# A two-phase convolution and FFN kernel: two images packed into one convolution, and the last image's search, broadcast and additions rearranged

## The reference, cut to what matters

```python
x = x + relu(batchnorm(conv3x3(sign(ln_c(x)), sign(w) * alpha) + b))   # ln_c over channels, batch statistics over all images
t = tokens(x)                                  # (32, 3136, 128)
s = ln_t(t)
weights = s @ wr + br                          # one router weight per token
sel = top (k - 1) of weights, k = 3136 / 2     # per image
t = t + s + (gelu(s[sel] @ w1 + b1) @ w2 + b2) * weights[sel]   # the last term for chosen tokens alone
```

## Time and profile before

| | us |
|---|---|
| median of 3 runs | 2095.73 |
| lowest, highest | 2092.15, 2099.53 |
| the profiled execution | 2102.06 |
| its span | 2100.1 |
| TensorE, VectorE, ScalarE, GpSimd busy | 1961.1, 1600.5, 1216.2, 938.0 |
| first convolution pass begins | 19.9 |
| last convolution pass ends | 471.5 |
| last matmul of the second phase ends | 2079 |

### The profile page before, as it was taken

The page is one execution under the profiler, slowest core; times in us unless marked ns, Lnnn a source line. Parts: engine busy times, 40 slices in busy tenths (PEclk is TensorE's granted clock), DMA queues, the critical chain, the costliest instruction groups (busy, mean ns, idle before and its releaser), DMA issues.

```text
span 2100.1 us, 35007 instructions
## 1 busy us (share of the span) xinstructions
PE 1961.1 (93%) x9515; PEld 961.7 (46%) x9515; DVE 1600.5 (76%) x4580; ACT 1216.2 (58%) x2030; POOL 938.0 (45%) x714
## 2 busy tenths in 40 slices
PE   6999999994999999999999999999999999999995
PEld 2444444442444444444444444444444444444442
DVE  4766666665788888888888888887888888878875
ACT  3555555544666666666666666666656666655652
POOL 1000000005465565566555566655656566555543
PEclk9999999996999999999999999999999999999998
DMA  6787877852133333333333333333333333333223
GB/s 251 279 297 283 301 291 288 295 215 73 52 141 117 115 116 132 114 126 117 126 112 135 116 112 120 135 113 113 130 119 117 123 115 122 116 112 129 96 76 119
DMA packets 78097, 318.24 MB, mean 152 GB/s; under 512 B 23561, under 2 KB 28610, under 8 KB 74050
## 3 DMA queue, kind: packets, MB, share of 16 engines
q1 hardware_dynamic: 64626, 265.07, 34.5%
q10 hardware_dynamic: 13392, 52.33, 6.7%
HBM read 237.88 MB, written 78.26 MB: 151 GB/s over the span
## 4 chain that ended last, share of the span: by engine, by line
PE 48%; DMA 11%; SPq 6%; DVE 4%; issue 4%; POOL 1%; ACT 1%; ACTq 0%; POOLq 0%; DVEq 0%
PE ps L1063 24%; DMA y<-y_int 6%; PE ps L1052 6%; PE ps L1054 5%; PE ps L1053 5%; PE ps L1008 5%; SPq L429 4%; DMA w_row<-wrow 3%; PE ps L1041 2%; DMA wse<-w_row 2%; SPq L435 1%; POOL rm L489 1%; ACT hs L566 1%; SPq L440 1%; DVE rm L776 1%
## 5 line engine op out<-in xcount | busy, mean ns | idle before, releaser
L1063 PE MATMUL ps<-hs,w_c 128*128 128x448 f32 x1792 | 765.1, 555 | 0.6 <-ACT yo L576 0.6
L566 ACT ACTIVATE hs<-ps,b1c,undo 128x448 f32<-128x448 f32 x896 | 609.3, 719 | 129.0 <-PE ps L1054 125.3
L1063 PEld LDWEIGHTS ps<-hs,w_c 128*128 128x128 f32 x1792 | 314.6, 191 | 211.3 <-issue 177.2
L965 PE MATMUL ps<-yo,cwT 128*128 128x448 bf16 x2016 | 396.2, 357 | 3.9 <-ACT y L544 3.9
L470 POOL TENSOR_TENSOR xb<-xb,zr 128x448 f32<-128x448 f32 x224 | 261.1, 1168 | 271.9 <-ACT zr L594 254.9
L475 POOL TENSOR_TENSOR tl<-tr,th 128x448 f16<-128x448 f32 x224 | 245.4, 1097 | 306.9 <-PE ps L1054 185.8
L1052 PE MATMUL ps<-th,w_h 128*128 128x448 f16 x896 | 318.7, 356 | 25.3 <-ACT hs L566 25.3
L1054 PE MATMUL ps<-th,w_l 128*128 128x448 f16 x896 | 316.3, 353 | 0.0
L1053 PE MATMUL ps<-tl,w_h 128*128 128x448 f16 x896 | 316.3, 353 | 0.0
L482 POOL TENSOR_TENSOR yo<-yo,base 128x448 f32<-128x448 f32 x224 | 281.3, 1262 | 77.4 <-DVE yo L885 77.4
L965 PEld LDWEIGHTS ps<-yo,cwT 128*128 128x128 bf16 x2016 | 193.8, 98 | 214.4 <-issue 24.9
(11 more groups left out here) (143 smaller groups left out, 2086.1 us busy)
## 6 DMA issues: line engine op xcount, KB each, us to landing
xb<-x SPq DMA_DIRECT2D x21, 1568.0 KB, 7.4
xb<-x SPq DMA_DIRECT2D x33, 896.0 KB, 4.7
gate_all<-gate_row ACTq DMA_DIRECT2D x32, 896.0 KB, 4.5
result<-yo SPq DMA_DIRECT2D x32, 896.0 KB, 3.5
y_int<-y SPq DMA_DIRECT2D x32, 784.0 KB, 4.1
xb<-x SPq DMA_DIRECT2D x33, 672.0 KB, 4.4
gate_all<-gate_row ACTq DMA_DIRECT2D x32, 672.0 KB, 5.6
result<-yo SPq DMA_DIRECT2D x32, 672.0 KB, 3.0
```

Of the source, the lines that this page charges most:

```text
L566: nc.scalar.activation(hs[(b + slot) % 2][:, j, :], ps[:, H_BANK + j, 0:T], ACT.Gelu_apprx_tanh, bias=b1c[:, j:j + 1], scale=undo[:, 1:2]) ...
L965: last = M(bank, cwT[:, t, :], sg[b][:, c * ROWS + dy:c * ROWS + dy + ROWS, dx:dx + SIDE], start=t == 0, stop=t == TAPS - 1)
L1063: last = M(bank, w2_c[:, j, :], hs[(b + c) % 2][:, j, :], start=first, stop=final)
```

## The change

First phase: the loop goes over 16 pairs of images. The signs of the two images are packed as second * 3072 + first into one padded fp32r frame; one convolution of nine fp32r passes per chunk gives 3072 * y2 + y1. ScalarE rounds the result / 3072 to int16 (y2), VectorE takes y1 = v - 3072 * y2 as fp16. All images of pairs 0 and 1, and of later pairs chunks 4 to 6, are centred by an fp32 matmul; chunks 0 to 3 of later pairs by subtracting a mean as before, chunks 0 to 2 on GpSimd and chunk 3 on VectorE. GpSimd also adds the two signs (the packing), after ScalarE has scaled one of them by 3072. Three PSUM banks hold convolution results. x and y move in two parts per image, y into one DRAM tensor for even images (fp16) and one for odd ones (int16). The phase is written out for all 16 pairs.

```diff
+PACK = 3072.0
+MEAN_FROM = 2
+MEAN_SLOT = 2
+V_RING = 3
-        cwT = sb("cwT", [C, TAPS, C], bf16)
+        cwT = sb("cwT", [C, TAPS, C], f32r)
+        packs = [sb(f"packs{b}", [C, PAD * PAD], f32r) for b in range(2)]
-        xs = [xb[0], xb[1], base[1]]
+        xs = [xb[0], xb[1], base[0], base[1]]
# TensorE
+            def centre(q, c):
+                for k in (1, 0):
+                    if k and (c == 0 or c == HALF):
+                        pe.wait_ge(x_in_s[q % 2][c // HALF], 32 * (q // 2 + 1))
+                    before = centred_before(q, c)
+                    if before[0] >= 0:
+                        pe.wait_ge(signed, signs_upto(*before, k))
+                    M(ps[:, CEN_BANK + k, 0:T], kt[:, K_CEN:K_CEN + C], cut(xs[(2 * q + k) % 4], c),
+                      start=True, stop=True).then_inc(centred, 1)
+            def conv(p, c):
+                chunk = p * NCH + c
+                pe.wait_ge(packed, p * NCH + min(c + 2, NCH))
+                wait_count(pe, decoded, chunk - V_RING + 1)
+                bank = ps[:, V_BANK + chunk % V_RING, 0:T].rearrange("p (r w) -> p r w", w=SIDE)
                 for t in range(TAPS):
                     dy, dx = divmod(t, 3)
+                    last = M(bank, cwT[:, t, :], pk[p % 2][:, c * ROWS + dy:c * ROWS + dy + ROWS, dx:dx + SIDE],
                              start=t == 0, stop=t == TAPS - 1)
+            for p in range(NP):
                 for c in range(NCH):
+                    conv(p, c)
+                    for q, d in centres_at(p, c):      # pair 0: its own chunks 4 to 6 and all of pair 1; else (p + 1, c), c >= 4
+                        centre(q, d)
+                    if c == (MEAN_SLOT if p else NCH - 1) and MEAN_FROM <= p + 2 < NP:
+                        token_means(p + 2)              # 4 chunks of both images
# GpSimd
+            for q in range(NP):
+                for c in range(NCH):
+                    if q >= MEAN_FROM and c < HALF - 1:
+                        for k in (1, 0):
+                            level(2 * q + k, c)
+                    if c:
+                        pack(q, c - 1)                  # waits for both signs, the scaled copy and the frame
+                pack(q, NCH - 1)
# ScalarE
+            def sign(q, c):                             # waits levelled or centred, and packed of two chunks before
+                for k in (1, 0):
+                    ...
+                    nc.scalar.activation(sgn[k][chunk % 2][:, :], z, ACT.Sign).then_inc(signed, 1)
+                act.wait_ge(signed, signs_upto(q, c, 1))
+                nc.scalar.activation(sgn[1][chunk % 2][:, :], sgn[1][chunk % 2][:, :], ACT.Copy,
+                                     scale=PACK).then_inc(scaled, 1)
+            for p in range(NP):
                 for c in range(NCH):
+                    for q, d in signs_at(p, c):         # (p + 1, c - 1); at c = 0 (p, 6)
+                        sign(q, d)
+                    take_high(p, c)                     # y2: waits conv_done, y_saved and bn_taken of the pair before
# VectorE
+            def decode(p, c):
+                dve.wait_ge(high_taken, chunk + 1)
+                ...
+                V.scalar_tensor_tensor(cut(y16[0], c), cut(y16[1], c), -PACK, ps[:, V_BANK + chunk % V_RING, 0:T],
+                                       ALU.mult, ALU.add).then_inc(decoded, 1)
# SyncE, per pair: load_pair(p + 2, 1); store_y(p - 1, 1); save_mean of both images of pair p + 2; store_y(p, 0); load_pair(p + 3, 0)
```

```diff
-NORM_AT = [31, 39, 51, 54, 63, 72, 74]
+NORM_AT = Steps([31, 39, 51, 54, 63, 72, 74], last=[31, 39, 51, 54, 63, 68, 72])
-ROUTER_AT = [26]
+ROUTER_AT = Steps([26], last=[20])
-COUNT_AT = [36, 39, 43, 46, 50, 53, 56, 61]
+COUNT_AT = Steps([36, 39, 43, 46, 50, 53, 56, 61], last=[30, 33, 36, 39, 42, 45, 48, 51])
-MASK_AT = 67
-SCAN_AT = 68
-OUT_AT = [25, 28, 31, 34, 38, 44, 49]
-GATE_OUT_AT = 17
+MASK_AT = Steps([67], last=[54])
+SCAN_AT = Steps([68], last=[55])
+OUT_AT = Steps([25, 28, 31, 34, 38, 44, 49], last=[7, 8, 9, 10, 11, 12, 13])
+GATE_OUT_AT = Steps([17], last=[0])
+                    if is_int(n) and n == n_img:        # SyncE, behind the store of the gate
+                        sp.wait_ge(gate_saved, n * 16)
+                        sp.wait_ge(gated, (n - 1) * NCH)
+                        spread_gates(sp, n - 1)
+            def add_late(m, b, c):                      # VectorE, chunks 4 to 6 of the last image
+                dve.wait_ge(gated, m * NCH + c + 1)
+                V.tensor_tensor(cut(yo[b], c), cut(yo[b], c), cut(base[b], c), ALU.add).then_inc(late_ready, 1)
```

More of the change, by code:

```diff
@@ L214, in block_kernel @@
         border_clear = sem("border_clear")
-        x_in_s = [sem(f"x_in{b}") for b in range(3)]
+        x_in_s = [[sem(f"x_in{b}_{part}") for part in range(2)] for b in range(2)]
+        packed = sem("packed")
+        scaled = sem("scaled")
+        high_taken = sem("high_taken")
+        decoded = sem("decoded")
         mean_done = sem("mean_done")
@@ L218, in block_kernel @@
         mean_saved = sem("mean_saved")
[L219 removed]
+        mean_in = [sem(f"mean_in{b}") for b in range(4)]
         levelled = sem("levelled")
[L221 to L222 removed]
+        levelled_last = sem("levelled_last")
         centred = sem("centred")
@@ L225, in block_kernel @@
         conv_done = sem("conv_done")
-        y_copied = sem("y_copied")
         bn_taken = sem("bn_taken")
-        y_saved = [sem(f"y_saved{b}") for b in range(2)]
+        y_saved = [sem(f"y_saved{part}") for part in range(2)]
         coef_ready = sem("coef_ready")
@@ L368, in _ @@
                              ).then_inc(params_in, 16)
+            for part in range(2):
+                load_pair(1, part)
             def load_x(n, b, part):
@@ L486, in phase2 @@
                 for pos in range(POS):
-                    for m, mb, _ in due(VAR_AT + 1, 1, n, b, pos):
+                    for m, mb, _ in due(VAR_AT.later(1), 1, n, b, pos):
                         pool.wait_ge(var_ready, m + 1)
@@ L497, in phase2 @@
                         low_part(m, mb, c)
-                    for m, mb, c in due([p + 1 for p in OUT_AT], -1, n, b, pos):
-                        add_base(m, mb, c)
+                    for m, mb, c in due(OUT_AT.later(1), -1, n, b, pos):
+                        if not (is_int(m) and m == n_img - 1 and c >= HALF):
+                            add_base(m, mb, c)
             pairs(pool, phase2, *P2, -2, n_img + 1)
@@ L680, in _ @@
+            phase1(0)
             dve.wait_ge(params_in, 16 * N_PARAMS)
@@ L893, in phase2 @@
                         choose(m, r)
-                    for m, mb, _ in due(COUNT_AT[0] - 1, 0, *at):
+                    for m, mb, _ in due(COUNT_AT.start(-1), 0, *at):
                         count_above(m, 0)
@@ L911, in phase2 @@
                         apply_gate(m, mb, c)
+                        if is_int(m) and m == n_img - 1 and c >= HALF:
+                            add_late(m, mb, c)
                     for m, mb, r in rounds:
                         next_candidate(m, r)
-                    for m, mb, _ in due(ROUTER_AT[-1] + 1, 0, *at):
+                    for m, mb, _ in due(ROUTER_AT.later(1), 0, *at):
                         take_router(m)
@@ new lines, in token_means @@
+            def token_means(q):
+                pe.wait_ge(x_in_s[q % 2][0], 32 * (q // 2 + 1))
+                for k in range(2):
+                    done = 2 * q + k - 2 * MEAN_FROM
+                    if done > 1:
+                        pe.wait_ge(mean_copied, done - 1)
+                    for c in range(HALF):
+                        last = M(ps[c * COLS:(c + 1) * COLS, MEAN_BANK + k, 0:T],
+                                 kt[:, K_MSEL + COLS:K_MSEL + 2 * COLS], cut(xs[(2 * q + k) % 4], c),
+                                 start=True, stop=True)
+                    last.then_inc(mean_done, 1)
```

445 lines of the change are left out of this document (227 added, 218 removed).

## The result

| | before | after |
|---|---|---|
| median, us (4 runs each, side by side) | 2096.05 | 2014.11 |
| lowest, highest | 2092.15, 2099.53 | 2012.59, 2015.51 |
| the profiled execution | 2102.06 | 2015.51 |
| its span | 2100.1 | 2013.7 |

The ratio is 0.9609, with a 95% interval of 0.9591 to 0.9628: 82 us faster. That is the predicted side, but 41 us short of the predicted 1973 and 8 us above the range.

What follows compares the result with a forecast made beforehand. TensorE was taken to bound both phases; first phase -118.5, handover +1 and last image -5 gave -122.5 us, from the median 2095.73 to 1973. Its own range was 1953 to 1990, with rivals A and B 1953 to 2006.

Steps and rivals of the forecast that it cites:

- handover: Between first and second phase: a decoding and one more statistic in the path, +1 us.
- last image: End of second phase: earlier router and counts, moved broadcast and additions, together -5 us (-1 to -8).
- DMA: First phase: 6.65 MB a pair at 370 GB/s takes 18.0 us, hidden by little under TensorE's time.
- I put 0.5 us of such waits on a pair: First phase: TensorE's waits in the chain between engines, added to its 19.1 us to give 19.6 a pair.
- Rival A: First phase: another engine's chain sets the pair at 22 us, total 2004; chance 0.11.
- Rival B: First phase: half-size stores of y drop full DMA use to 320 GB/s, pair 20.8 us, total 1989; chance 0.08.
- The pass: First-phase convolution: an fp32r pass takes 0.20 us, bounds 0.192 and 0.22; 12.6 us a pair.
- Centring and means: First phase, TensorE: centring 0.376 a pass, 4.5 us a pair plus 0.3 for changes of kind; means 1.7.
- Begin of the phase: First convolution at 27 us, pair 0 ends at 58.5, late means cost 7 to 9 once, pair 1 ends at 87.
- Router: Last image: router moved up by 6 positions runs 3.4 us sooner.
- additions: Last image: three of seven final additions moved from GpSimd to VectorE end 1.3 us sooner.
- broadcast on SyncE: Last image: broadcast on SyncE instead of ScalarE priced at zero, 0.5 us if the stores of image 30 are late.

Runs made afterwards that it cites:

- e7: Kernel after, with stores of y from pair 1 on cut to 64 columns a part (1.5 MB a pair left out): 1996.3 us, ratio 0.9498.
- e5: Kernel after, with SyncE storing both means, waiting once, then issuing both broadcasts: 2001.8 us, ratio 0.9531.
- e10: Kernel after, with both means stored before both broadcasts and stores of y cut to 64 columns a part: 1995.8 us, ratio 0.9515.
- e2: Kernel after, with frame and convolution weights in fp16 and a packing factor of 1536: 2015.3 us, ratio 0.9589.
- e11: Kernel after, with a second pair of y buffers for odd pairs from pair 5 on: 2014.2 us, ratio 0.9595.
- e4: Kernel after, with every chunk centred on TensorE by fp32 matmuls and no token means: 2028.7 us, ratio 0.9639.
- e13: Kernel after, with the early aggregate of batch statistics taken over 2 groups instead of 210: 2015.3 us, ratio 0.9596.
- e8: Kernel after, with the last image's three additions moved back from VectorE to GpSimd: 2016.1 us, ratio 0.9613.
- e12: Kernel after, with second y buffers, means stored together and first half of x loaded from ScalarE's queue: 2001.3 us, ratio 0.9530.

## Why the prediction was wrong, step by step

Between the two profiled spans -86.4 us lie where -122.5 were forecast. By stages, missing or won against the forecast: the third means come at 99.5 and not at 92.4, which is the forecast end of pair 1, 87, and 27 passes (+7); eleven pairs at 22.25 instead of 19.6 (+29); from there to the last pass 50.5 instead of 45, which is 353 - 92.4 - 11 x 19.6 (+5.5); handover 9.4 after 8.0, so +1.4 for +1; last image -6.2 for -5 (-1); and the middle of the second phase, which the change doesn't touch, came out 4.9 shorter, as much as it scatters by (1519 to 1533 us in the profiles). The first phase alone is 42 short, and the rest gives 6 of them back.

**The failed step is *DMA*: "18.0 us. It is hidden, by little."** Measured, it isn't hidden: TensorE stands 21.3 of 240 us for x, 2.0 a pair. I compared a mean throughput with TensorE's sum. The mean itself was right (303 GB/s at a share of 0.83 are 365 at full use, for the forecast 370). What holds TensorE isn't the sum of the bytes but when the one load that it needs may start and what is in flight with it. x of pair p+3 can't be asked for before the signs of pair p+1 have freed its buffer, the token means of the next pair need all of its first part, and in the 12.65 us from issue to landing the other parts of x and both stores of y keep the engines full. The trace of before had parts of that sum: the copy-to-broadcast way of 3.3 us, which SyncE now goes twice in a row, and 4.5 us to land for an 896 KB broadcast. I used both rows once, for pair 1, and not in the steady pair. e7 (fewer bytes) and e5 (no second round trip ahead of the load) shorten the loop in two ways and both give time; e10 takes both, and nine of eleven pairs become the forecast 19.6 to 19.9. e2 and e11 exclude the passes and the y buffers as what sets the steady pair; e4 shows that TensorE's own work takes just its sum where no x is waited for.

**"I put 0.5 us of such waits on a pair"** stands for the chain of engines, and there it held, partly by luck: in e10, without DMA waits, nine pairs are 19.6 to 19.9, but 19.4 of that is TensorE's own work (63 x 0.211 + 4.5 + 1.6) and not 19.1, so the waits were less than 0.5. The 2.65 us that a pair took more were, but for the 0.6 of the passes, waits; these were of a kind that the sum had no term for.

**One block on VectorE** had no term either: the preparation of the second phase, 9.6 us behind pair 2, which makes one pair of e10 25.0 us long. In the kernel after the same pair takes 25.0 and ends with a wait for x of 3.7 us, so there the two delays overlap, and how much of the 29 us is this block's no run tells; by e10 it would be left, some 5 us once, when x no longer binds.

**Rival A** isn't seen in the window: no wait of TensorE there ends with ScalarE or VectorE.

**Rival B** named the right resource (DMA sets the pair, gaps after a load of x) but by throughput: full use down to 320 GB/s for the halves of y. On average that reason was wrong, with 365 at full use. But the stretch at 203 to 205 has 219 GB/s at full engines, and e7, with the stores of y short, 333 in its like: the stores of y do slow the engines, as B said, in the very stretch in which x is on its way. That it is their smaller packets isn't shown; no run stores y whole. Its price of 1.2 us a pair was too low for the loop's 2, and with 0.08 it had too little chance.

**The pass**: 0.211, between my 0.20 and the upper bound of 0.22. Row 387.01 below has 36 passes in 7.82 us, so (7.82 - 0.38)/35 = 0.213; four centring passes and 45 of the convolution take 10.98 us from 358.24 to 369.22, and 3.40 with nine, so (10.98 - 3.40)/36 = 0.211. Loads are 0.193 long, so load and a rest of 0.02 would make the period. That fits e2, where load and pass are both shorter, but e2 changes the type too, and no run has the one without the other. It cost 0.6 us a pair, 8 in all; by e2, twice as much given back changed nothing while x was waited for.

```profile
387.01 7.82 PE L1074 MATMUL ps<-packs,cwT 128*128 128x448 f32 x36 [1.74 <-DVE y16a L759]
```

The Trainium skill (TensorE: Matmul & The Clock Gate, Weight-path perf modes) says that the fast load is for types other than FP32, and leaves fp32r open. This case's trace shows it for 128 x 128 weights: an fp32r load takes 0.193 us as an fp32 one does (0.191 at L1168), and a bf16 one 0.098.

**Centring and means**: 0.375 a pass and 1.64 us for 16 mean passes, as forecast; the 0.3 us for changes of kind are zero (e4), which by luck made up for half of the pass.

**Begin of the phase**: first pass at 27.02 (forecast 27), end of pair 0 at 59.0 (58.5). The means formed in pair 1 would by the forecast come at 64 (58.5 and 27 passes) with a wait of 7 to 9 us behind them; they come at 78.0, and those formed in pair 2 are 7 us late:

```profile
57.29 1.71 PE L1062 MATMUL ps<-xb,kt 128*32 128x448 f32 x16
...
78.00 3.21 PE L1062 MATMUL ps<-base,kt 128*32 128x448 f32 x16 [8.98 <-DMA base<-x]
```

I had TensorE wait at convolution 4 for late levelling; it waits before that, for x: the stores of both means, then those of y (65.18), then the load (66.12), which lands at 78.0. It is the same queue.

**Last pairs**: +5.5, which I had no term for. One gap of 1.7 us stands behind the early aggregate (5.84 us of VectorE); e13 closes it. Another, of 1.6 us in the kernel after and up to 4.2 in the others, is the one in which e13 has ScalarE wait 3.0 us for the stores of y. The same stretch scatters by 4 us between runs that don't differ there, so more of it can't be told apart.

**Last image**: all steps held in sign and size. Router 3.9 earlier (3.4), search and mask 0.9 shorter (0.6), additions 1.4 by e8 (1.3; its terms as written, 9.86 - 4 x 1.4 - 5 x 0.55, give 1.5), broadcast on SyncE 0.1 (0). By the Trainium skill's exclusive lock (SBUF — State Buffer, two separate sides) the additions would have brought 1.6, an estimate in the prediction; e8's 1.4 lies between that and mine and doesn't decide. That TensorE stands behind the first count didn't reach the end, as said.

The range was too narrow at the top: A and B were priced singly, at 2.4 and 1.2 us a pair, and the measured mechanism, with the pass, cost 2.65 and a begin and an end besides. At the bottom it was too wide: passes of 0.192 and no waits are 1.0 us a pair, 13 in 13 pairs and not 18.

## What to carry to other kernels

When a change takes nearly a third off the bound engine's work per pair (27.6 to 19.4 us here) and leaves the bytes nearly as they are, don't compare bytes per stage with time per stage; walk the loop of the load that this engine needs: when its buffer comes free, what stands ahead of it in its queue, and what shares the engines until it lands. The mean DMA share doesn't answer this: it was 0.79 in the kernel before without a wait of TensorE, 0.83 in the kernel after with 21 us of waits in 240, and 0.87 in e12's five pairs with 2.4 in 102. Then look for round trips in the loading queue (store, wait, read back): issuing both stores before waiting once took 12 us off here without touching any engine's work. And look again behind the stage that you made faster, for blocks that stand there once, as VectorE's preparation did.

## What the runs showed of the hardware that I hadn't expected

- Full DMA engines have no one rate: 420 to 435 GB/s in slices of 2.75 us, 219 behind the stores of y, 365 as the mean of the window scaled to full use. The Trainium skill (SBUF — State Buffer, the bandwidth-pool section) gives a core some 358 GB/s from HBM and its 16 DMA engines 436. The slices come up to the second; since they count reads, writes and broadcasts together, they don't show whether loads alone pass the first.
- fp32r passes with 448 columns came every 0.211 us, and not 0.187 (448/2.4 GHz) or the 0.192 of bf16 and fp16 ones. Their loads of 0.193 fit as the cause; no run separates them from the type.
- An addition on VectorE beside one on GpSimd takes 1.43 us where it takes 0.62 alone (2006.42 and 2008.42 above): in the last image the last GpSimd addition and the first of VectorE's still collide, once.
- The granted clock goes with TensorE's waits: 0.96 over the window with 21 us idle, 1.00 in e4 with none, 0.94 in e2 with 30. Where it falls, the work behind the wait takes longer: the 16 mean passes took 1.71 us at 192.41 (clock 1.00) and 2.74 at 214.60 (0.60 over the row, so mostly the lower level of 1.2 GHz), 1 us more. Not every wait brings it: behind 2.55 us at 258.03 and 2.93 at 301.67 the same passes took 1.71. Part of what a wait costs is this.
